# Gram results copied out of PSUM by ScalarE and VectorE, half the partitions each

## The chip, the cores and the metric

The program runs on one core of a Trainium2 chip. The metric is the device time of one execution, in microseconds. Each kernel is executed several times, and the median is compared.

## The reference

For each of 2048 samples there are 27 vectors of 128 numbers. The kernel must compute all 351 products of two different vectors of a sample, put them behind the first vector, and run the result through five dense layers, all in float32:

```python
bottom_mlp_output = bottom_output[:, 0, :]                       # (2048, 27, 128) -> (2048, 128)
interaction = jnp.einsum('bnd,bmd->bnm', bottom_output, bottom_output)
interaction_flat = interaction[:, _TRIL_R, _TRIL_C]              # 351 pairs
x = jnp.concatenate([bottom_mlp_output, interaction_flat, zero_pad], axis=1)
x = jax.nn.relu(x @ W0.T + b0)      # 480 -> 1024
x = jax.nn.relu(x @ W1.T + b1)      # -> 1024
x = jax.nn.relu(x @ W2.T + b2)      # -> 512
x = jax.nn.relu(x @ W3.T + b3)      # -> 256
return x @ W4.T + b4                # -> 1
```

## The kernel before

The samples are worked on in four chunks of 512. Before the main part, `first_gram` makes the pair products of chunk 0. Then come four bodies, `body(c)` for c from 0 to 3. Body c runs the dense layers of chunk c on TensorE, and between their matmuls it makes the pair products (grams) of chunk c+1. Body 3 has no next chunk, so it has no grams.

Every float32 operand of a dense layer is split in a high and a low float32r part. One product of a weight tile and a 128x512 activation tile is three matmuls, at lines 687, 688 and 689 (`product`). VectorE makes the splits: `split` is two instructions at lines 592 and 594, from what `relu` on ScalarE (line 414) wrote.

The grams of a chunk are made in 16 slices of 32 samples, and each slice in two halves, so 32 halves h = 0 to 31 in each of bodies 0 to 2. A half is `gram_half` on TensorE: four matmuls at line 712, which fill the two PSUM banks `gps`. There is one `gps` for all halves, so half h+1 may not start before the results of half h have been copied out. The four useful blocks of a result lie on the partition quadrants 0, 32, 64 and 96, each at another column, so that copying out takes four instructions of 32 partitions: `grams_from_psum` on ScalarE, line 382, which counts up the semaphore `grams_out`.

VectorE's share of a half is `half_point`. At an even half it is `input_parts` (lines 506 and 508: the split of the slice that is needed three slices later). At an odd half it is `half_sum` (line 524), and after every fourth slice, at h = 7, 15, 23 and 31, also `pair_products`: a transpose (line 555), two sums (559, 565) and `choose_pairs` (534). Later `transpose_pairs` on TensorE (line 725) turns these pairs, and `pairs_hi_part` (ScalarE) and `pairs_lo_part` (VectorE, line 583) move them from the PSUM bank gps to the features of the next chunk.

The order of work on every engine is written out by hand, and every engine takes its own list in order. In layer 0 a half stands behind each of the output tiles 2 to 7 (h = 0 to 5). In layer 1 the places are given by product (tile m, input tile k; k = 8 lies in the middle of the layer 2 products that follow tile m):

```python
L1_HALVES = [[1, 3, 5, 7], [0, 2, 7], [0, 3, 6, KT1], [0, 2, 7], [0, 2, 4, 7], [0, 2, KT1], [0, 2, 4, 6, KT1]]
TURNS = {(1, 4): 0, (3, 4): 1, (5, 5): 2, (MT1 - 1, 6): 3}
```

So h = 6, 7, 8 and 9 stand behind products 1, 3, 5 and 7 of tile 0, h = 10, 11 and 12 in tile 1, and so on. `layer2(c, m - 1, ...)` with its four products of m - 1 follows each tile m from 1 on. `interleave` gives ScalarE and VectorE the same order: at a place first the half, then the turn, then the output tile if k = 7.

GpSimd takes part in body 0 only: `w1_lo`, line 346, makes the low parts of the layer 1 weights, eight times.

Of the kernel before, what the change touches and what calls it, by code (L numbers as in the profile page):

```python
# [6 lines left out]
BATCH, INPUTS, EMB = 2048, 27, 128  # L7
SIZES = [1024, 1024, 512, 256]
P = 128
# [4 lines left out]
GROUP = 4  # L14
QUAD = P // GROUP
SLICE_GROUPS = 8
HALF_GROUPS = SLICE_GROUPS // 2
SCOLS = SLICE_GROUPS * GROUP * INPUTS
EVEN = INPUTS + INPUTS % 2
GCOLS = GROUP * EVEN  # L20
BANK = 512
SLICES_SUB = SUB // (GROUP * SLICE_GROUPS)
SLICES = SUBS * SLICES_SUB
HALVES = 2 * SLICES
# [38 lines left out]
def rec_program(nc, x_t, x0_t, w0, w1, w2, w3, w4, biases, b4, out):  # L63
# [5 lines left out]
    with ctx:  # L69
        def sb(name, shape, dt=f32):  # L70
            return ctx.enter_context(nc.sbuf_tensor(name, shape, dt))

        def sem(name):
            return ctx.enter_context(nc.semaphore(name))
# [28 lines left out]
        grams2 = sb("grams2", [P, 2, SLICE_GROUPS, 2, INPUTS])  # L103
# [16 lines left out]
        gps = ctx.enter_context(nc.psum_tensor("gps", [P, 2, BANK], f32))  # L120
# [13 lines left out]
        xpad_done = sem("xpad_done")  # L134
        xh_done, xl_done = sem("xh_done"), sem("xl_done")
        gram_done, grams_out, half_sums = sem("gram_done"), sem("grams_out"), sem("half_sums")
        turned_done, sums_done, pairs_done = sem("turned_done"), sem("sums_done"), sem("pairs_done")
        pairs_t, pairs_hi, pairs_lo = sem("pairs_t"), sem("pairs_hi"), sem("pairs_lo")
        dense_hi, dense_done = sem("dense_hi"), sem("dense_done")
# [6 lines left out]
        def ge(eng, s, value):  # L146

            if not (isinstance(value, int) and value <= 0):
                eng.wait_ge(s, value)
# [15 lines left out]
        def parts(g, p):  # L165

            return SLICES * (g - 1) + p + 1
# [58 lines left out]
        def pair_bank(first):  # L226
            return acc[:, 2, :] if first else gps[:, 0, :]
# [142 lines left out]
        def _(act):  # L370
            def grams_from_psum(g, h):

                n = HALVES * g + h
                act.wait_ge(gram_done, n + 1)
                if h % 2 == 0 and h >= 4:
                    act.wait_ge(half_sums, SLICES * (g - 1) + h // 2 - 1)
                at = h % 2 * HALF_GROUPS
                for q in range(GROUP):
                    rows = slice(q * QUAD, (q + 1) * QUAD)
                    src = gps[rows].rearrange("p b (g w) -> p (b g) w", w=2 * P)[:, :, 0:2 * GCOLS]  # L380
                    src = src.rearrange("p g (t c) -> p g t c", c=GCOLS)
                    last = act.activation(grams2[rows, h // 2 % 2, at:at + HALF_GROUPS, :, :],  # L382
                                          src[:, :, :, q * EVEN:q * EVEN + INPUTS], ACT.Copy)
                last.then_inc(grams_out, 1)
# [77 lines left out]
            def body(c, more):  # L462
                def on_half(h):
                    if more:
                        grams_from_psum(c + 1, h)

                def on_turn(s):
                    if more:
                        pairs_hi_part(c + 1, s)

                def on_tile(layer, m):
                    relu(c, layer, m, work[:, m % 2, :])
                    if c == 0 and layer == 0 and m < EARLY + 2:
                        w1_hi(m - EARLY)

                def after_tile(m):
                    if c == 0 and m + 2 < MT1:
                        w1_hi(m + 2)

                interleave(on_half, on_turn, on_tile, after_tile)  # L480
                for m in range(MT2):
                    relu(c, 2, m, acc[:, m, :])
                if more:
                    relu(c + 1, 0, 0, work[:, 0, :])
                for m in range(MT3):
                    relu(c, 3, m, acc[:, m, :], more)
                if more:
                    relu(c + 1, 0, 1, work[:, 1, :])
# [8 lines left out]
        def _(dve):  # L497
# [3 lines left out]
            def input_parts(g, p):  # L501
                n = SLICES * g + p
                hi, lo = xs[:, p % XSLOTS, 0, :, 0:INPUTS], xs[:, p % XSLOTS, 1, :, 0:INPUTS]
                dve.wait_ge(x_in[p % XSLOTS], 16 * (SLICES // XSLOTS * g + p // XSLOTS + 1))
                ge(dve, gram_done, 2 * (n - XSLOTS + 1))
                dve.tensor_copy(hi, by_sample(xraw, p)).then_inc(xh_done, 1)  # L506
                dve.wait_ge(xh_done, parts(g, p))
                dve.tensor_tensor(lo, by_sample(xraw, p), hi.bitcast(f32), ALU.subtract).then_inc(xl_done, 1)  # L508

            def dense_parts(g):  # L510
# [4 lines left out]
                dve.tensor_tensor(featL[:, 0, :], x0raw[:, :], featH[:, 0, :].bitcast(f32), ALU.subtract)\  # L515
                   .then_inc(dense_done, 1)

            def half_sum(g, p):

                n = SLICES * g + p  # L520
                dve.wait_ge(grams_out, 2 * (n + 1))
                ge(dve, turned_done, SUBS * g + p // SLICES_SUB)
                at = p % SLICES_SUB * SLICE_GROUPS
                dve.scalar_tensor_tensor(out=grams[:, at:at + SLICE_GROUPS, :], in0=grams2[:, p % 2, :, 0, :],  # L524
                                         scalar=0.5, in1=grams2[:, p % 2, :, 1, :], op0=ALU.mult, op1=ALU.add)\
                   .then_inc(half_sums, 1)
# [23 lines left out]
            def pair_products(g, s):  # L550

                n = SUBS * g + s
                dve.wait_ge(half_sums, SLICES_SUB * (n + 1 - SUBS))
                dve.wait_ge(sums_done, 2 * n)
                dve.transpose(turned[:, :, :], grams[:, :, :].rearrange("p g m -> p m g")).then_inc(turned_done, 1)
                dve.wait_ge(turned_done, n + 1)
                dve.wait_ge(pairs_done, n)
                full = turned[:, :, 0:INPUTS]
                dve.tensor_tensor(sums[:, 0:INPUTS * INPUTS].rearrange("p (i j) -> p i j", j=INPUTS),
                                  full, full.rearrange("p i j -> p j i"), ALU.add).then_inc(sums_done, 1)  # L560

                v = turned[:, 0, 0:APART]
                above = bass.AP(v.tensor, v.offset + APART + 1, [v.ap[0], (QUAD + 1, APART)])
                below = bass.AP(v.tensor, v.offset + QUAD * (APART + 1), [v.ap[0], (QUAD + 1, APART)])
                dve.tensor_tensor(sums[:, INPUTS * INPUTS:], above, below, ALU.add).then_inc(sums_done, 1)
                choose_pairs(n)

            def half_point(g, h):

                p = h // 2  # L570
                if h % 2 == 0:
                    if p + AHEAD < SLICES:
                        input_parts(g, p + AHEAD)
                else:
                    half_sum(g, p)
                    if p % SLICES_SUB == SLICES_SUB - 1:
                        pair_products(g, p // SLICES_SUB)
# [60 lines left out]
            def body(c, more):  # L638
                def on_half(h):
                    if more:  # L640
                        half_point(c + 1, h)
# [42 lines left out]
        def _(pe):  # L684
# [18 lines left out]
            def gram_half(g, h, turned_before):  # L703

                n, p = HALVES * g + h, h // 2
                pe.wait_ge(xl_done, parts(g, p))
                pe.wait_ge(grams_out, n)
                pe.wait_ge(pairs_lo, SUBS * g + turned_before)
                for j in range(HALF_GROUPS):
                    k = h % 2 * HALF_GROUPS + j  # L710
                    four = slice(k * GROUP, (k + 1) * GROUP)
                    last = pe.matmul(gps[:, j // 2, j % 2 * 2 * P:j % 2 * 2 * P + 2 * GCOLS],  # L712
                                     xs[:, p % XSLOTS, 0, four, :].rearrange("p b n -> p (b n)"),
                                     xs[:, p % XSLOTS, :, four, 0:EVEN], start=True, stop=True)
                last.then_inc(gram_done, 1)

            def transpose_pairs(g, s, halves_before, first=False):

                pe.wait_ge(pairs_done, SUBS * g + s + 1)
                if first:  # L720
                    ge(pe, pairs_lo, s)
                else:
                    pe.wait_ge(grams_out, HALVES * g + halves_before)
                for t in range(PAIR_TILES):
                    last = pe.transpose(pair_bank(first)[0:PAIRS_TILE, t * SUB:(t + 1) * SUB],  # L725
                                        pairs[:, t * PAIRS_TILE:(t + 1) * PAIRS_TILE], ident[:, :])
                last.then_inc(pairs_t, 1)
# [84 lines left out]
            for m in range(LEFT_AFTER, MT0 - 1):  # L812
                layer0_left(m)
            transpose_pairs(0, SUBS - 1, 0, True)
            layer0_left(MT0 - 1)

# [77 lines left out]
```

## Time and profile before

| | before |
|---|---|
| median of 3 runs | 526.73 us (525.83 to 528.72) |
| profiled execution, its own time | 528.12 us |
| its span, first to last instruction | 526.3 us |
| TensorE busy | 492.3 us, 94% |
| VectorE busy | 299.4 us, 57% |
| ScalarE busy | 239.6 us, 46% |
| GpSimd busy | 44.1 us, 8% |
| mean granted TensorE clock | 0.981 |

The engine names in the profile are PE for the matmuls and PEld for the weight loads of TensorE, DVE for VectorE, ACT for ScalarE, POOL for GpSimd. A row of the timeline gives the start within the span, the duration, the engine and the line of the kernel. Some 1.8 us of the profiled execution's time lie outside its span. A row with x4 is four instructions one right behind the other. Matmuls are pipelined, so their durations overlap, and the distance from start to start is what a matmul takes of TensorE's time.

### The profile page before, as it was taken

The page shows a single profiled execution, that of the slowest core. Times are in us where ns is not written, and L with a number is a line of the kernel's source. Part 1 is how long each engine was busy: PE and PEld are TensorE (multiplying, and loading weights), DVE is VectorE, ACT ScalarE, POOL GpSimd, SP SyncE. Part 2 cuts the span into 40 slices and gives each one's busy share as a digit, 9 for nine tenths or more (in the row PEclk, how much of TensorE's full clock was granted, in tenths as well). Part 3 has the DMA queues.
Part 4 walks back from the last instruction along what each step waited for, and adds up shares of the span by engine and source line. Part 5 has one row for each costly group of instructions (what it writes and reads, how often), then busy time and mean ns, then how long its engine had stood idle before and what let it go on. Part 6 is the DMA issues. An engine that isn't in the chain of part 4 may idle for free.

```text
span 526.3 us, 6672 instructions
## 1 busy us (share of the span) xinstructions
PE 492.3 (94%) x2480; PEld 402.8 (77%) x2480; DVE 299.4 (57%) x455; ACT 239.6 (46%) x579; POOL 44.1 (8%) x27
## 2 busy tenths in 40 slices
PE   6999769897999999899999999899999999999996
PEld 5999766675777878687777878687787888888874
DVE  3596897867545756757554666767464634101124
ACT  2887266574663335645554425745645322101111
POOL 0336340130310000000000000000000000000000
PEclk9999779999999989999999999999999999999998
DMA  7895046566537322454344232354332200424200
GB/s 272 327 375 182 7 128 222 176 220 230 181 130 244 106 63 70 153 192 158 149 142 154 81 101 68 127 203 147 112 128 81 81 1 0 141 100 161 80 0 2
DMA packets 17456, 72.28 MB, mean 137 GB/s; under 512 B 2448, under 2 KB 2448, under 8 KB 13328
## 3 DMA queue, kind: packets, MB, share of 16 engines
q1 hardware_dynamic: 17424, 71.86, 38.8%
q8 instruction: 20, 0.33, 0.3%
q14 instruction: 12, 0.10, 0.1%
HBM read 63.45 MB, written 8.40 MB: 137 GB/s over the span
## 4 chain that ended last, share of the span: by engine, by line
PE 77%; DVE 10%; issue 7%; ACT 4%; DMA 1%; SPq 0%; DVEq 0%; ACTq 0%
PE work L687 15%; PE work L688 15%; PE work L689 15%; PE gps L712 9%; PE acc L687 6%; PE acc L688 6%; PE acc L689 6%; PE acc L699 2%; DVE xs L506 1%; ACT grams L382 1%; ACT grams L398 1%; DMA xraw<-x_t 1%; DVE h2h L592 1%; PE gps L699 1%; PE gps L725 1%
## 5 line engine op out<-in xcount | busy, mean ns | idle before, releaser
L382 ACT ACTIVATE grams<-gps 32x216 f32<-32x216 f32 x384 | 131.0, 341 | 82.0 <-PE gps L712 78.4
L687 PE MATMUL work<-h1h,w1s 128*128 128x512 f32 x256 | 102.4, 400 | 0.0
L688 PE MATMUL work<-h1h,w1s 128*128 128x512 f32 x256 | 101.7, 397 | 0.0
L689 PE MATMUL work<-h1l,w1s 128*128 128x512 f32 x256 | 100.8, 394 | 0.0
L414 ACT ACTIVATE act_out<-work,bias 128x512 f32<-128x512 f32 (+1 forms) x64 | 42.3, 662 | 116.3 <-PE work L689 111.7
L712 PEld LDWEIGHTS gps<-xs 128*128 128x128 f32 x384 | 54.6, 193 | 38.9 <-issue 27.3
L712 PE MATMUL gps<-xs 128*128 128x224 f32 x384 | 62.3, 285 | 17.0 <-issue 9.6
L687 PE MATMUL work<-featH,w0l 117*128 117x512 f32 (+5 forms) x160 | 59.9, 374 | 4.0 <-ACT act_out L421 3.7
L592 DVE CAST h2h<-act_out 128x512 fp32r<-128x512 f32 x40 | 19.2, 481 | 75.7 <-ACT act_out L414 75.7
L524 DVE SCALAR_TENSOR_TENSOR grams<-grams 128x216 f32<-128x216 f32 x48 | 20.3, 422 | 73.5 <-ACT grams L382 72.7
L689 PE MATMUL work<-featL,w0h 117*128 117x512 f32 (+5 forms) x160 | 58.5, 366 | 0.0
L688 PE MATMUL work<-featH,w0h 117*128 117x512 f32 (+5 forms) x160 | 58.5, 366 | 0.0
L689 PEld LDWEIGHTS work<-h1l,w1s 128*128 128x128 f32 x256 | 48.1, 188 | 11.3
L508 DVE TENSOR_TENSOR xs<-xraw,xs 128x864 fp32r<-128x864 f32 x48 | 55.0, 1145 | 1.7
L687 PEld LDWEIGHTS work<-h1h,w1s 128*128 128x128 f32 x256 | 48.4, 189 | 8.6
L688 PEld LDWEIGHTS work<-h1h,w1s 128*128 128x128 f32 x256 | 48.4, 189 | 8.0
L687 PE MATMUL acc<-h2h,w2l 128*128 128x512 f32 x128 | 50.7, 396 | 0.0
L688 PE MATMUL acc<-h2h,w2h 128*128 128x512 f32 x128 | 50.7, 396 | 0.0
L689 PE MATMUL acc<-h2l,w2h 128*128 128x512 f32 x128 | 50.5, 395 | 0.0
L592 DVE CAST h1h<-act_out 128x512 fp32r<-128x512 f32 (+1 forms) x48 | 21.5, 448 | 41.9 <-ACT act_out L414 41.8
L687 PEld LDWEIGHTS work<-featH,w0l 117*128 117x128 f32 (+2 forms) x160 | 32.8, 205 | 8.3 <-ACT act_out L421 4.1
L688 PEld LDWEIGHTS work<-featH,w0h 117*128 117x128 f32 (+2 forms) x160 | 33.0, 206 | 4.0
(68 smaller groups left out, 582.4 us busy)
## 6 DMA issues: line engine op xcount, KB each, us to landing
xraw<-x_t SPq DMA_DIRECT2D x64, 432.0 KB, 5.1
w1s<-w_parts SPq DMA_DIRECT2D x24, 1024.0 KB, 4.8
w_parts<-w1s SPq DMA_DIRECT2D x8, 1024.0 KB, 5.7
stage<-w_t SPq DMA_DIRECT2D x8, 512.0 KB, 7.1
w0raw<-w_t SPq DMA_DIRECT2D x4, 512.0 KB, 7.2
w2raw<-w_t SPq DMA_DIRECT2D x4, 512.0 KB, 6.5
x0raw<-x_t SPq DMA_DIRECT2D x4, 256.0 KB, 3.6
w3raw<-w_t SPq DMA_DIRECT2D x1, 512.0 KB, 6.6
```

What stands on the lines that cost most here:

```text
L382: last = act.activation(grams2[rows, h // 2 % 2, at:at + HALF_GROUPS, :, :], src[:, :, :, q * EVEN:q * EVEN + INPUTS], ACT.Copy)
L398: last = act.activation(dst, src[:, :, :, q * INPUTS:(q + 1) * INPUTS], ACT.Copy)
L414: act.activation(act_out[:, slot(layer, m, more), cols], bank[:, cols], ACT.Relu, bias=bias[:, row:row + 1]).then_inc(relu_done, 1)
L506: dve.tensor_copy(hi, by_sample(xraw, p)).then_inc(xh_done, 1)
L508: dve.tensor_tensor(lo, by_sample(xraw, p), hi.bitcast(f32), ALU.subtract).then_inc(xl_done, 1)
L524: dve.scalar_tensor_tensor(out=grams[:, at:at + SLICE_GROUPS, :], in0=grams2[:, p % 2, :, 0, :], scalar=0.5, in1=grams2[:, p % 2, :, 1, :] ...
L592: dve.tensor_copy(hi, full).then_inc(hi_done, 1)
L687: pe.matmul(dst, wl, ah, start=start, stop=False)
L688: pe.matmul(dst, wh, ah, start=False, stop=False)
L689: return pe.matmul(dst, wh, al, start=False, stop=stop)
L699: last = pe.matmul(first_banks(p)[:, k // HALF_GROUPS, at:at + GROUP * INPUTS], four.rearrange("p b n -> p (b n)"), four[:, :, 0:INPUTS], ...
L712: last = pe.matmul(gps[:, j // 2, j % 2 * 2 * P:j % 2 * 2 * P + 2 * GCOLS], xs[:, p % XSLOTS, 0, four, :].rearrange("p b n -> p (b n)"), x ...
```

## The change

ScalarE copies only the quadrants 0 and 32 of a half. The quadrants 64 and 96 are copied by VectorE, in the new `lower_from_psum`, which is the first thing in `half_point`. A new semaphore `lower_out` counts the copied halves. `gram_half`, `transpose_pairs` and `half_sum` now wait for it as well as for `grams_out`. The pair products of chunk 0 (`first_from_psum`) keep their four copies on ScalarE.

```diff
         gram_done, grams_out, half_sums = sem("gram_done"), sem("grams_out"), sem("half_sums")
+        lower_out = sem("lower_out")
...
             def grams_from_psum(g, h):
...
-                for q in range(GROUP):
+                for q in range(GROUP // 2):
...
+            def lower_from_psum(g, h):
+
+                n = HALVES * g + h
+                dve.wait_ge(gram_done, n + 1)
+                if h % 2 == 0 and h >= 4:
+                    dve.wait_ge(half_sums, SLICES * (g - 1) + h // 2 - 1)
+                at = h % 2 * HALF_GROUPS
+                for q in range(GROUP // 2, GROUP):
+                    rows = slice(q * QUAD, (q + 1) * QUAD)
+                    src = gps[rows].rearrange("p b (g w) -> p (b g) w", w=2 * P)[:, :, 0:2 * GCOLS]
+                    src = src.rearrange("p g (t c) -> p g t c", c=GCOLS)
+                    last = dve.tensor_copy(grams2[rows, h // 2 % 2, at:at + HALF_GROUPS, :, :],
+                                          src[:, :, :, q * EVEN:q * EVEN + INPUTS])
+                last.then_inc(lower_out, 1)
+
             def half_sum(g, p):
 
                 n = SLICES * g + p
                 dve.wait_ge(grams_out, 2 * (n + 1))
+                dve.wait_ge(lower_out, 2 * (n + 1 - SLICES))
...
             def half_point(g, h):
 
                 p = h // 2
+                lower_from_psum(g, h)
...
             def gram_half(g, h, turned_before):
...
                 pe.wait_ge(grams_out, n)
+                ge(pe, lower_out, n - HALVES)
...
             def transpose_pairs(g, s, halves_before, first=False):
...
                     pe.wait_ge(grams_out, HALVES * g + halves_before)
+                    pe.wait_ge(lower_out, HALVES * (g - 1) + halves_before)
```

## Rows read from the trace of the kernel before

**Rows 1.** The page, part 1: busy time of each engine.

```profile
PE 492.3 (94%) x2480; PEld 402.8 (77%) x2480; DVE 299.4 (57%) x455; ACT 239.6 (46%) x579; POOL 44.1 (8%) x27
```

**Rows 2.** The page, part 4: the chain that ended last, by engine.

```profile
PE 77%; DVE 10%; issue 7%; ACT 4%; DMA 1%; SPq 0%; DVEq 0%; ACTq 0%
```

**Rows 3.** The page, part 5: busy, mean ns, idle time before.

```profile
L382 ACT ACTIVATE grams<-gps 32x216 f32<-32x216 f32 x384 | 131.0, 341 | 82.0 <-PE gps L712 78.4
```

**Rows 4.** Timeline, TensorE, body 1: start us, us, engine, line, operands, [idle before].

```profile
199.03 0.60 PE L712 MATMUL gps<-xs 128*128 128x224 f32 x4
199.47 0.40 PE L687 MATMUL work<-featH,w0l 128*128 128x512 f32 x1
...
202.28 0.60 PE L712 MATMUL gps<-xs 128*128 128x224 f32 x4
...
211.06 0.68 PE L712 MATMUL gps<-xs 128*128 128x224 f32 x4 [0.26 <-issue]
...
213.28 0.68 PE L712 MATMUL gps<-xs 128*128 128x224 f32 x4
213.79 0.40 PE L687 MATMUL work<-h1h,w1s 128*128 128x512 f32 x1
...
215.49 0.68 PE L712 MATMUL gps<-xs 128*128 128x224 f32 x4
...
279.78 0.68 PE L712 MATMUL gps<-xs 128*128 128x224 f32 x4
```

**Rows 5.** Timeline, ScalarE, the same stretch.

```profile
213.99 1.40 ACT L382 ACTIVATE grams<-gps 32x216 f32<-32x216 f32 x4 [0.81 <-PE gps L712]
```

**Rows 6.** Timeline, VectorE, the same body.

```profile
215.43 0.38 DVE L524 SCALAR_TENSOR_TENSOR grams<-grams 128x216 f32<-128x216 f32 x1 [2.44 <-ACT grams L382]
...
219.84 0.60 DVE L506 CAST xs<-xraw 128x864 fp32r<-128x864 f32 x1
...
221.46 0.38 DVE L524 SCALAR_TENSOR_TENSOR grams<-grams 128x216 f32<-128x216 f32 x1
221.75 0.42 DVE L592 CAST h2h<-act_out 128x512 fp32r<-128x512 f32 x1
...
222.82 0.42 DVE L513 CAST featH<-x0raw 128x512 fp32r<-128x512 f32 x1
...
223.88 0.60 DVE L506 CAST xs<-xraw 128x864 fp32r<-128x864 f32 x1
```

**Rows 7.** Groups by form: VectorE's read of PSUM.

```profile
L583 DVE TENSOR_TENSOR featL<-gps,featH 117x384 fp32r<-117x384 f32 x12 | 6.6, 554 | 3.9 <-ACT featH L406 3.8
```

**Rows 8.** Timeline, body 0: VectorE's end and the TensorE group that it released.

```profile
124.35 0.55 DVE L583 TENSOR_TENSOR featL<-gps,featH 117x384 fp32r<-117x384 f32 x1
125.05 0.68 PE L712 MATMUL gps<-xs 128*128 128x224 f32 x4 [1.98 <-DVE featL L583]
```

**Rows 9.** Timeline, body 0: VectorE beside a GpSimd subtraction.

```profile
94.22 2.54 POOL L346 TENSOR_TENSOR w1s<-stage,w1s 128x1024 fp32r<-128x1024 f32 x1 [18.86 <-ACT w1s L440]
...
94.39 2.64 DVE L592 CAST h2h<-act_out 128x512 fp32r<-128x512 f32 x1
...
116.87 2.43 DVE L565 TENSOR_TENSOR sums<-turned 128x13 f32<-128x13 f32 x1
...
141.78 3.08 DVE L559 TENSOR_TENSOR sums<-turned 128x729 f32<-128x729 f32 x1
```

**Rows 10.** Timeline, TensorE, starts behind its two longest idle times before body 3.

```profile
56.23 0.58 PE L687 MATMUL work<-featH,w0l 128*128 128x256 f32 x1 [3.70 <-ACT act_out L421]
...
70.92 1.17 PE L712 MATMUL gps<-xs 128*128 128x224 f32 x4 [4.07 <-issue]
```

**Rows 11.** Windows: us, PE busy, PEld, DVE, ACT, POOL, PEclk, DMA share, GB/s.

```profile
56.00:62.00 6.00, 5.76 (x27) 5.77 (x28) 4.34 (x10) 2.70 (x6) 1.30 (x1) 0.50 0.00 0
...
71.00:76.00 5.00, 5.00 (x24) 5.00 (x25) 4.97 (x4) 3.44 (x9) 4.18 (x2) 0.50 0.28 91
...
125.00:127.00 2.00, 1.96 (x11) 1.71 (x12) 0.00 (x0) 1.20 (x4) 0.00 (x0) 1.00 1.01 419
```

## Prediction

> **What bounds the kernel now.** I read the page's busy times first, then the chain, then the costliest groups, and then the timeline around the halves. TensorE is busy 94% of the span [rows 1] and is 77% of the chain that ended last [rows 2], so only what moves TensorE's matmuls moves the end. The copies that the change touches are ScalarE's largest group: 384 instructions, 131.0 us, 341 ns each [rows 3]. ScalarE is busy under half of the time, so its total says nothing. The question is which wait ends last before a half starts on TensorE.
>
> A half that waits for nothing has its next product 0.44 us behind its start (199.03 to 199.47), and one that had to wait has it at 0.51 (213.28 to 213.79), so a wait costs 0.07 beyond its own length [rows 4]. A matmul of 512 columns takes 0.234 start to start: a layer 0 tile has twelve of them, from 199.47 to 202.28 [rows 4]. So a product takes 0.70, and from 213.79 two of them end at 215.19. The next half starts only at 215.49: a stall of 0.30 [rows 4]. ScalarE's four copies begin at 213.99, 0.71 behind the half's start, and end at 215.39, 0.10 before the next half [rows 5]. So where only two products lie between halves, the four copies (1.40) set the pace, and the half waits. In body 1 I count 15 such stalls, from the half at 211.06 to that at 279.78, with the two turns at tiles 1 and 3: thirteen of 0.28 to 0.34, one of 0.42 and one of 1.00 (h = 10, with only one product before it), 5.69 us in all, and with 15 x 0.07 = 1.05 it is **6.7 us per body**. VectorE makes TensorE wait in none of them. Body 2 shows the same pattern. This is all that halving ScalarE's copies can win there: 2 x 0.35 instead of 4 x 0.35 would end 0.70 earlier, more than the 0.30 that is missing.
>
> **What the change costs on VectorE.** Two copies of 216 elements per half are added, 192 in all. None of the trace's rows is a plain copy from PSUM by VectorE. From PSUM it took 554 ns for 384 elements [rows 7]; from SBUF the same number of elements as ours, 216, took 0.38 (line 524) [rows 6]. With one element per cycle as in rows of this kind, (0.554 - 0.38) / 168 = 1.04 ns an element, both rows lie on one line, and so I take 0.38. Between instructions I add 0.04 (my choice; on ScalarE it is 0.01, 1.40 / 4 against 0.341 [rows 3, 5]), so a pair costs 0.84. Low bound: a single-source copy inside SBUF runs faster, 0.42 for 512 elements and 0.60 for 864 [rows 6], by which slope one of 216 takes 0.27, about 0.30 with its gap. High bound: 0.50 each, near the whole 0.55 of the longer PSUM read.
>
> The Trainium skill (VectorE: DVE Perf Modes, "Why PSUM operands drop a tier") says that a float32 operand in PSUM keeps a copy at one element per cycle, which rules out my low bound; no run here shows it yet. Its cycle table ("The TRN2 errata" section) gives (120 + 216) / 0.96 = 350 ns as an estimate, with which a body would lose some 6 us in place of the 8 below.
>
> **Where VectorE stands when a half is ready.** This decides. `lower_from_psum` stands in VectorE's own order, behind everything that earlier places gave it, and the half after next cannot start before it. Its other work per place, start to start [rows 6]: `half_sum` 0.30 (221.46 to 221.75); `half_sum` and `pair_products` together 4.41 (215.43 to 219.84); `input_parts` 1.62 (219.84 to 221.46); `split` 1.07 (221.75 to 222.82); the dense parts 1.06 (to 223.88). Before, a half did not wait for any of it except for inputs made three slices ahead. From VectorE's end to the half it releases are 0.15 (124.90 to 125.05) [rows 8], so from the end of the pair's 0.84 slot 0.11.
>
> I write R for the time at which a half's results are ready, 0.71 behind its start. With n products between, the next half could start at R - 0.20 + 0.70 n.
>
> *Halves 7 to 11* (two products apart, h = 10 one). At h = 6 VectorE copies (0.84) and splits an input (1.62), so it reaches half 7 at V, 0.62 late, and half 8 is held to V + 0.95, a stall of 0.36. Then VectorE does copy 7 (0.84), sum and pair products (4.41), copy 8 (0.84): 6.09, and half 9 starts at V + 6.20. Free it would start at V + 0.95 + 1.91 = V + 2.86. **Stall 3.34.** Next, input parts 1.62 and copy 9: half 10 at V + 8.66 against 7.41, stall 1.25. Then sum, the split of tile (1,0), the dense parts, copy 10 (0.30 + 1.07 + 1.06 + 0.84): half 11 at V + 11.93 against 10.57, stall 1.36. Then input parts and copy 11: the turn at V + 14.39 against 13.84, stall 0.55.
>
> *Halves 15 to 18.* After half 15 VectorE does copy, sum, pair products, the split of tile (1,2), copy 16: 7.16, and half 17 starts at R + 7.27. TensorE has three products, half 16, three products: free at R + 4.44. **Stall 2.83**, and 0.55 at half 18 behind the next input parts.
>
> *Halves 23 to 25.* The same chain, 7.27, against five products, a half, two products: 5.14. **Stall 2.13.**
>
> *The rest.* Half 6 stands two products behind the last tile of layer 0, whose relu and split VectorE must do before copy 5: 1.40 by the same account. Half 22 gets 0.36, as half 8. Half 31's pair products have eight products before the turn needs them, no stall. In layer 0 a tile and a half take 3.25, and VectorE needs per pair of them 2 x (1.07 + 0.84) + 1.62 + 0.30 = 5.74 of 6.50: covered. All others are covered too, since ScalarE's 0.70 and VectorE's 0.84 then both fit.
>
> Sum: 1.40 + 0.36 + 3.34 + 1.25 + 1.36 + 0.55 + 2.83 + 0.55 + 0.36 + 2.13 = 14.1, and ten times 0.07: **14.8 us per body against 6.7 now, +8.1**. So the stalls of 0.30 mostly go, and fewer but long ones come. The same account with a copy at 0.30 gives +5.0, with 0.50 +11.2. It needs no idle VectorE on average: the engine is 57% busy [rows 1] and stays under 70%.
>
> **Body 0** has the same three places and more. GpSimd's subtractions hold VectorE instructions: the cast at 94.39 took 2.64 instead of 0.42, ending with GpSimd's at 96.76, the sum at 116.87 took 2.43 instead of some 0.17, that at 141.78 took 3.08 instead of 1.51 [rows 9]. The second and third lie inside pair products 1 and 2 and the first between copies 9 and 10, so all three (2.2 + 2.2 + 1.6 = 6.0) now stand before a half; some 1 us of it costs already (the 1.98 of idle at 125.05 [rows 8]). The Trainium skill (SBUF — State Buffer, "Who interferes with whom") says VectorE and GpSimd hold a shared port pair against each other for whole instructions, and that a one-source instruction outside the two-port modes is not held: then the new copies themselves are not, only what stands before them. Layer 0 there has 256 columns, a tile and half took 2.2, VectorE's 5.1 per pair of tiles exceeds 4.4: +1.2 over four tiles. Together 8.1 + 6.0 - 1.0 + 1.2 = 14.3.
>
> **The clock.** Behind idle times of 3.70 and 4.07 [rows 10] the granted clock was 0.50 (1.2 GHz) for at least 6 and 5 us; behind 1.98 it stayed 1.00 (2.4 GHz) [rows 8, 11]. At half clock at most half the time is lost: some 2.5 us an event. In body 0 the stall at half 17 becomes 2.8 + 2.2 = 5, so I add one event: +2.2, taking the part of it that matmuls fill. Whether 3.34 in the steady bodies does it, no row tells; it lies between the two. I leave it out of the sum. The Trainium skill (TensorE: Matmul & The Clock Gate, "The HAM clock gate") also has the clock at half behind an idle stretch, as rows 10 and 11 show.
>
> **Sum.** 2 x 8.1 + 14.3 + 2.2 = 32.7. On the profiled execution, 528.1 + 32.7 = 560.8 (span 559); on the median, which is 1.4 lower, **559 us**.
>
> **Rivals.**
> - *A: as forecast, and the clock falls in bodies 1 and 2 too*, behind half 9 at least: 2 x 2.5 more, with a second event in body 0 some 567.
> - *B: the copies collide.* Both engines read the same two banks at once. If one waits for the other, the pair takes up to 0.70 longer. By the account's slope (3.1 us a body for 0.16 us a pair), 3 x 13 more: about 597. Nothing in the trace has both engines on `gps` at once; that they read different partitions speaks against it.
> - *C: faster.* VectorE would be in time at the halves, and then only the 6.7 us a body go: 527 - 20 = 507. For it: VectorE is idle 43% of the span and idled 2.44 before 215.43 [rows 6]. Against: it idles elsewhere than at pair products. It decides in favour of C only if the chain of 6.09 behind half 7 takes under 2.8, that is if pair products were under 0.8 instead of some 4.0, or stood behind the next halves' copies.
> - *D: no change*, gains equal to losses: it needs the long stalls at a fourth of their size, at most 3.5 us a body beside the small ones. Only copies at nearly no time and half the chain would do that.
>
> **How the numbers follow.** The forecast (546 to 563) 0.70, A 0.17, B 0.04, C 0.04, D 0.02, and slower by less than forecast 0.03. Low end: copies at 0.30 and body 0 at 9, 2 x 5.0 + 9 = 19: 546; I go to 544. High end: copies at 0.50 with the clock of A, 2 x (11.2 + 2.5) + 22 = 49: 576. Faster or slower means by over 0.5%, 2.6 us, about what a measurement of this kernel can tell from no change.
>
> **What would show it.** ScalarE's line 382 halves to 192 instructions and some 65 us. VectorE has 192 new copies of about 0.38. In body 1 TensorE has idle times before line 712 of about 3.2, 2.7 and 2.0 us at halves 9, 17 and 25, released by VectorE, and the 0.30s at halves 7, 21, 28, 29 and 30 are gone. If the copies took under 0.2, or if TensorE did not wait behind pair products, the prediction would be wrong. The last body and everything before the first half must be as long as before.

## The result and the profile after

The changed kernel takes 574.9 us (median of 4 runs, 573.59 to 575.65) against 527.3 us (4 runs): a ratio of 1.090, 95% interval 1.086 to 1.094. It is slower by 48 us. The forecast was 559 with a range of 544 to 576, so the time lies in the range, 1 us below its upper end, and above the 546 to 563 that had the largest chance. The profiled execution took 573.59 us, with a span of 571.8 and a mean granted clock of 0.933 instead of 0.981.

Part 1 and three groups of part 5 of the page of the changed kernel:

```profile
PE 508.8 (89%) x2480; PEld 420.9 (74%) x2480; DVE 377.3 (66%) x647; ACT 174.2 (30%) x387; POOL 44.4 (8%) x27
...
L383 ACT ACTIVATE grams<-gps 32x216 f32<-32x216 f32 x192 | 65.3, 340 | 173.4 <-PE gps L731 172.0
...
L731 PE MATMUL gps<-xs 128*128 128x224 f32 x384 | 67.0, 301 | 47.0 <-DVE grams L530 46.8
...
L530 DVE COPY grams<-gps 32x216 f32<-32x216 f32 x192 | 73.8, 384 | 39.7 <-PE gps L731 36.5
```

Against [rows 1, 3], ScalarE's copies are halved in number and no slower (340 ns, before 341). VectorE's are 192 of 384 ns. VectorE is 66% busy, so it is not full. But TensorE now idles 47.0 us before the halves (line 731), and 46.8 of it end with a VectorE copy.

The timeline shows how. TensorE in body 1 of the changed kernel, the halves 6 to 10 (starts 233.53, 235.45 for half 7, 237.83 for half 8, 243.19 for half 9 and 245.73 for half 10) and then halves 17 and 25; and half 25 of body 2:

```profile
233.53 0.68 PE L731 MATMUL gps<-xs 128*128 128x224 f32 x4 [1.49 <-DVE grams L530]
...
237.83 0.68 PE L731 MATMUL gps<-xs 128*128 128x224 f32 x4 [0.29 <-DVE grams L530]
...
243.19 1.17 PE L731 MATMUL gps<-xs 128*128 128x224 f32 x4 [3.27 <-DVE grams L530]
...
245.73 1.17 PE L731 MATMUL gps<-xs 128*128 128x224 f32 x4
...
271.30 1.17 PE L731 MATMUL gps<-xs 128*128 128x224 f32 x4 [2.95 <-DVE grams L530]
...
299.13 0.68 PE L731 MATMUL gps<-xs 128*128 128x224 f32 x4 [2.24 <-DVE grams L530]
...
430.24 0.76 PE L731 MATMUL gps<-xs 128*128 128x224 f32 x4 [2.25 <-DVE grams L530]
```

VectorE in the same stretch: copies of half 7, half sum, pair products (lines 572 to 551), copies of half 8:

```profile
236.79 0.78 DVE L530 COPY grams<-gps 32x216 f32<-32x216 f32 x2
237.66 0.38 DVE L541 SCALAR_TENSOR_TENSOR grams<-grams 128x216 f32<-128x216 f32 x1
238.08 1.95 DVE L572 STREAM_TRANSPOSE turned<-grams 128x864 f32<-128x864 f32 x1
240.06 1.41 DVE L576 TENSOR_TENSOR sums<-turned 128x729 f32<-128x729 f32 x1
241.39 0.17 DVE L582 TENSOR_TENSOR sums<-turned 128x13 f32<-128x13 f32 x1
241.60 0.52 DVE L551 COPY pairs<-sums 128x351 f32<-128x351 f32 x1
242.15 0.78 DVE L530 COPY grams<-gps 32x216 f32<-32x216 f32 x2
```

Half 8 was ready at 238.5, 0.71 behind its start at 237.83, but its copies on VectorE began only at 242.15, behind the pair products. Half 9 started 0.26 behind their end (242.93). And the half that started at 243.19 takes 1.17 instead of 0.68: TensorE is at half clock. The windows tell it (columns: stretch, us, busy of PE, PEld, DVE, ACT and POOL with counts, then PEclk, DMA share, GB/s); the first two follow halves 9 and 17 of body 1, the third half 25 of body 1, the fourth half 25 of body 2:

```profile
242.00:250.00 8.00, 6.74 (x22) 5.25 (x23) 7.57 (x16) 2.05 (x5) 0.00 (x0) 0.57 0.64 244
270.00:278.00 8.00, 6.70 (x24) 5.72 (x24) 5.82 (x12) 1.36 (x4) 0.00 (x0) 0.57 0.20 56
298.00:304.00 6.00, 4.87 (x25) 4.11 (x26) 4.22 (x9) 1.49 (x4) 0.00 (x0) 1.00 0.00 0
430.00:436.00 6.00, 5.76 (x22) 4.79 (x23) 3.35 (x6) 1.17 (x3) 0.00 (x0) 0.72 0.01 3
```

For the split of the loss I read from each timeline when the first half starts and when the first matmul of layer 4 starts in each body. Body 0 is from the first half, bodies 1 and 2 from layer 4 to layer 4:

| us | body 0 | body 1 | body 2 |
|---|---|---|---|
| before | 121.5 | 121.5 | 119.2 |
| changed | 142.7 (+21.2) | 133.7 (+12.2) | 131.9 (+12.7) |

From there to the last layer 4 both kernels take 94.8, and before the first half 64.8 and 64.5. So all the loss lies in the bodies that have halves. The kernel before takes 2.3 us more for body 1 than for body 2; there the windows show half clock for some 3.4 us right behind the layer 4 of body 0 (0.72 granted from 188 to 194), and none in body 2.

### The profile page after: what moved, and what is told of

Read it like the earlier page. It is cut to its first block and busy times, and to the rows that moved or that the text cites. A ratio compares the mean times of both kernels' runs of the same rounds, so it can differ in the third digit from the quotient of the medians.

```text
span 571.8 us, 6809 instructions
## 1 busy us (share of the span) xinstructions
PE 508.8 (89%) x2480; PEld 420.9 (74%) x2480; DVE 377.3 (66%) x647; ACT 174.2 (30%) x387; POOL 44.4 (8%) x27
## 5 line engine op out<-in xcount | busy, mean ns | idle before, releaser
L383 ACT ACTIVATE grams<-gps 32x216 f32<-32x216 f32 x192 | 65.3, 340 | 173.4 <-PE gps L731 172.0
L731 PEld LDWEIGHTS gps<-xs 128*128 128x128 f32 x384 | 60.7, 211 | 66.2 <-issue 60.5
L731 PE MATMUL gps<-xs 128*128 128x224 f32 x384 | 67.0, 301 | 47.0 <-DVE grams L530 46.8
L705 PE MATMUL work<-h1h,w1s 128*128 128x512 f32 x256 | 108.8, 425 | 0.0
L706 PE MATMUL work<-h1h,w1s 128*128 128x512 f32 x256 | 107.7, 421 | 0.0
L707 PE MATMUL work<-h1l,w1s 128*128 128x512 f32 x256 | 106.3, 415 | 0.0
L530 DVE COPY grams<-gps 32x216 f32<-32x216 f32 x192 | 73.8, 384 | 39.7 <-PE gps L731 36.5
L707 PEld LDWEIGHTS work<-h1l,w1s 128*128 128x128 f32 x256 | 51.9, 203 | 12.7
L610 DVE CAST h2h<-act_out 128x512 fp32r<-128x512 f32 x40 | 17.0, 424 | 65.6 <-ACT act_out L415 65.6
L705 PEld LDWEIGHTS work<-h1h,w1s 128*128 128x128 f32 x256 | 52.1, 204 | 9.3
L706 PEld LDWEIGHTS work<-h1h,w1s 128*128 128x128 f32 x256 | 52.2, 204 | 8.8
L610 DVE CAST h1h<-act_out 128x512 fp32r<-128x512 f32 (+1 forms) x48 | 19.2, 401 | 36.1 <-ACT act_out L415 36.1
```

The source lines that it names most:

```text
L530: last = dve.tensor_copy(grams2[rows, h // 2 % 2, at:at + HALF_GROUPS, :, :], src[:, :, :, q * EVEN:q * EVEN + INPUTS])
L610: dve.tensor_copy(hi, full).then_inc(hi_done, 1)
L705: pe.matmul(dst, wl, ah, start=start, stop=False)
L706: pe.matmul(dst, wh, ah, start=False, stop=False)
L707: return pe.matmul(dst, wh, al, start=False, stop=stop)
```

## The experiments

All are the changed kernel with one edit, except where said. Times are medians beside runs of the kernel before on the same chip (526.8, 527.8 and 526.9 in the three groups).

**1. Pair products cut short.** The pairs of chunks 1 to 3 are left out, and the instructions that would make them are kept short in place.

```diff
-                dve.transpose(turned[:, :, :], grams[:, :, :].rearrange("p g m -> p m g")).then_inc(turned_done, 1)
+                dve.transpose(turned[:, 0:1, :], grams[:, :, 0:1].rearrange("p g m -> p m g")).then_inc(turned_done, 1)
...
-                dve.tensor_tensor(sums[:, 0:INPUTS * INPUTS].rearrange("p (i j) -> p i j", j=INPUTS),
-                                  full, full.rearrange("p i j -> p j i"), ALU.add).then_inc(sums_done, 1)
+                dve.tensor_tensor(sums[:, 0:INPUTS], full[:, 0, :], full[:, 0, :], ALU.add).then_inc(sums_done, 1)
```

> The changed kernel, but pair_products works on one column group only: the transpose takes 1 of 27 blocks and the first sum 27 of 729 elements (so the pairs of chunks 1 to 3 are not computed; the other instructions, all waits and the places stay). Backlog theory (a half waits behind the 4 us of pair products in VectorE's order): the block shrinks from 4.0 to about 1.2 us, the stalls of 3.4, 3.1 and 2.4 us per body go, the clock stays at 1.00 in bodies 1 and 2, and the time falls from 575 to 525 to 535. Rival (the copies themselves or both engines reading the same banks cost it): most of the loss stays, 560 or more.

539.4 us, ratio 1.023 (1.020 to 1.027). The bodies take 130.1, 123.0 and 122.4: 35 of the 48 us are gone, though all 192 copies and all waits are still there. The expectation of 525 to 535 was too low by at least 4 us: body 0 keeps 8.6 of its loss, and bodies 1 and 2 keep 1.5 and 3.2. In body 1 half 9, the one that waited for pair products 0, is now at 224.81 (half 8 at 222.37, half 10 at 227.35):

```profile
222.37 0.68 PE L730 MATMUL gps<-xs 128*128 128x224 f32 x4 [0.31 <-DVE grams L530]
224.81 0.68 PE L730 MATMUL gps<-xs 128*128 128x224 f32 x4 [0.35 <-DVE grams L530]
227.35 0.68 PE L730 MATMUL gps<-xs 128*128 128x224 f32 x4 [1.15 <-DVE grams L530]
```

Idle 0.35 where it was 3.27. What stands ahead of the copies is the main cause, and the two engines' reading of the same banks is not.

**2. Copies cut short.** Each copy of VectorE takes 27 of its 216 elements, so most of the quadrants 64 and 96 is left uncopied.

```diff
-                    last = dve.tensor_copy(grams2[rows, h // 2 % 2, at:at + HALF_GROUPS, :, :],
-                                          src[:, :, :, q * EVEN:q * EVEN + INPUTS])
+                    last = dve.tensor_copy(grams2[rows, h // 2 % 2, at:at + 1, 0:1, :],
+                                          src[:, 0:1, 0:1, q * EVEN:q * EVEN + INPUTS])
```

> The changed kernel, but each of VectorE's copies takes 27 of its 216 elements (so the grams of partitions 64 to 127 are mostly not copied); the waits and the place in VectorE's order stay. Backlog theory: a pair costs about 0.44 instead of 0.84 us, the stalls at halves 9, 17 and 25 stay at about 2.8, 2.4 and 1.7 us since they are made of pair products, and the time is 545 to 558. Rival (the duration of 192 copies, 74 us on VectorE, is the cost): the time falls to that of before or below, 510 to 530.

552.1 us, ratio 1.048 (1.043 to 1.053), as the backlog theory had it. TensorE still idles 2.72, 2.39 and 1.72 before halves 9, 17 and 25 of body 1. With the copies cut short about half of the loss stays (25 of 48 us). The copies' own length matters too, since a late half waits for the pair products and for one or two pairs of copies behind them; so what experiments 1 and 2 win, 35 and 23 us, adds up to more than the loss. The page of this run also gives the price per element of a copy from PSUM:

```profile
L530 DVE COPY grams<-gps 32x27 f32<-32x27 f32 x192 | 36.0, 188 | 46.6 <-PE gps L731 43.5
```

The 189 elements fewer save 196 ns, 1.04 ns each.

**3. The split three to one at every half.** ScalarE copies three quadrants, VectorE one.

```diff
+        ON_VECTOR, FIRST_Q = [0, 1, 2, 3, 4, 5, 6, 7, 8, 9, 10, 11, 12, 13, 14, 15, 16, 17, 18, 19, 20, 21, 22, 23, 24, 25, 26, 27, 28, 29, 30, 31], 3
...
-                for q in range(GROUP // 2):
+                for q in range(FIRST_Q if h in ON_VECTOR else GROUP):
...
-                for q in range(GROUP // 2, GROUP):
+                for q in range(FIRST_Q, GROUP):
```

`ON_VECTOR` lists the halves of which VectorE takes a part, here all, and `FIRST_Q` is its first quadrant.

> The split is 3 to 1: at every half ScalarE copies quadrants 0 to 64 (1.05 us) and VectorE only quadrant 96. By my account with the measured 0.26 us from VectorE to TensorE a body loses 5.5 us in place of 9.6 on waits: half 9 still waits 3.1, half 17 2.8, half 25 2.1. With the clock falls and body 0's extra some 550 to 558. If VectorE's total time (a half less of copies, 37 us) were what counts, half of the loss would go: 551; if pair products ahead of copies count, no more than a third.

556.5 us, ratio 1.056 (1.052 to 1.061), in the range given. Before halves 9, 17 and 25 of body 1 TensorE idles 2.98, 2.73 and 2.06, against 3.27, 2.95 and 2.24 with two copies. The result does not tell the two readings named there apart: 40% of the loss is gone, between a third and a half, and bodies differ in clock falls as well. The three idle times speak for the queue: they fell by only 0.2 to 0.3 each.

**4. Pair products in two pieces.**

```diff
                 dve.transpose(turned[:, :, :], grams[:, :, :].rearrange("p g m -> p m g")).then_inc(turned_done, 1)
+
+            def pair_sums(g, s):
+
+                n = SUBS * g + s
...
                 lower_from_psum(g, h)
-                if h % 2 == 0:
+                if h % (2 * SLICES_SUB) == 1 and h > 1:
+                    half_sum(g, p)
+                    pair_sums(g, h // (2 * SLICES_SUB) - 1)
+                elif h % 2 == 0:
...
                         pair_products(g, p // SLICES_SUB)
+                        if h == HALVES - 1:
+                            pair_sums(g, SUBS - 1)
```

Here `pair_products` ends behind the transpose, and `pair_sums` is the rest of it.

> The changed kernel with pair_products cut in two: the transpose stays at halves 7, 15 and 23, the sums and the choice of pairs move behind the copies and the half sum of halves 9, 17 and 25. Same instructions. If the backlog of VectorE's work counts and not the length of one block, the stalls move (half 9 from 3.4 to 1.5, half 11 to some 3.4, half 17 from 3.1 to 1.0, the turns 1 and 2 up to 1.3 and 2.3) and their sum stays: 0.5 us less per body by my account, with one clock fall less per body 2 us more, so 566 to 573. If the block is the cause, the time falls to 550 or below.

567.5 us, ratio 1.077 (1.072 to 1.081), in the range given. The stalls moved. The halves 8, 9, 10 and 11 and the turn of body 1 (230.72, 233.99, 236.53, 241.97, 244.41; line 754 is the turn):

```profile
230.72 0.68 PE L740 MATMUL gps<-xs 128*128 128x224 f32 x4 [0.31 <-DVE grams L530]
233.99 0.68 PE L740 MATMUL gps<-xs 128*128 128x224 f32 x4 [1.19 <-DVE grams L530]
236.53 0.94 PE L740 MATMUL gps<-xs 128*128 128x224 f32 x4 [1.16 <-DVE grams L530]
241.97 0.68 PE L740 MATMUL gps<-xs 128*128 128x224 f32 x4 [1.91 <-DVE grams L530]
244.41 0.56 PE L754 MATMUL gps<-ident,pairs 128*117 128x128 f32 x3 [0.35 <-DVE grams L530]
```

Half 11 idled 1.91, less than the 3.4 I expected: I had not followed that with TensorE at half clock behind half 10 VectorE gets some time back. Cutting the block in two wins 7 us, not the loss, so the length of one block is not the cause. Body 1, with one clock fall, took 129.3; body 2, with two, 133.6. The fall in body 1 came behind half 10, with idle times of only 1.19 and 1.16 ahead of it (granted clock 0.52 from 237.0 to 240.3).

**5. Fillers for the clock.** Nine more matmuls ahead of halves 9, 17 and 25, in the time in which TensorE waits anyway. Their results are overwritten.

```diff
             def gram_half(g, h, turned_before):
...
+                if h in (9, 17, 25):
+                    m = {9: 0, 17: 3, 25: 5}[h]
+                    pe.wait_ge(relu_done, nth(g - 1, 1, m))
+                    for _ in range(9):
+                        pe.matmul(work[:, (m + 1) % 2, :], w0h[:, 0, 0:P], featH[:, 0, :], start=True, stop=True)
```

First with ten, at halves 9 and 17 only:

> The changed kernel with ten more matmuls of 512 columns on TensorE ahead of half 9 and of half 17, into the bank of work that is free there (their results are overwritten): they fill 2.3 of the 3.4 and 3.1 us that TensorE waits there anyway. If the half clock behind these waits is a cost of its own: the clock stays at 1.00 in bodies 1 and 2, some 2 to 3 us are won behind half 17, little behind half 9 because VectorE is late at halves 10 and 11 in any case, and the time is 562 to 570. If the stalls alone are the loss and the clock only goes with them: 574 to 576.

573.1 us, ratio 1.087 (1.082 to 1.092): outside what either reading gave, between their 570 and 574. The trace shows why. In body 1 half 25 came at 90.1 us behind the start of the body (the layer 4 of the body before) instead of 91.9, but the clock, full behind halves 9 and 17, now fell behind half 25, and from there to layer 4 it took 43.3 instead of 41.8. So about 3.4 us at half clock cost 1.5. Behind half 9 nothing was won: TensorE now idled 1.17 and 1.33 for VectorE before halves 10 and 11, which at half clock it had not. Then, with all three filled, beside the changed kernel itself:

> The changed kernel itself, unchanged, beside the next one on the same chip: 574 to 576.

> The changed kernel with nine extra 512-column matmuls ahead of half 9, half 17 and half 25 in each of bodies 0 to 2. With fillers at halves 9 and 17 only, TensorE came to half 25 of body 1 1.8 us earlier, but the clock then fell behind half 25 and took 1.5 back. If the clock is a cost of its own, the fall behind half 25 is gone too, and bodies 1 and 2 are each 2 to 3 us shorter than in the changed kernel: 567 to 571. If not: no change against it.

575.9 us for the changed kernel (ratio 1.093, 1.089 to 1.096) and 565.9 with the fillers (1.073, 1.069 to 1.076): 10 us, with 81 matmuls more, and 1 us below the 567 to 571 expected. Body 1 is shorter by 5.7 us and body 2 by 2.1, where 2 to 3 were given for each. The windows of body 1, first of the changed kernel on this chip, then with fillers:

```profile
205.60:341.50 135.90, 123.79 (x564) 100.19 (x564) 100.52 (x180) 38.46 (x91) 0.00 (x0) 0.92 0.34 116
```

```profile
203.60:333.90 130.30, 121.78 (x592) 98.05 (x592) 100.64 (x180) 38.43 (x91) 0.00 (x0) 1.00 0.35 121
```

With the clock at 1.00 in the whole body it takes 130.3. The halves 9, 10 and 11 of it stand much as the prediction's account has them, 1.33 and 1.50 late at 10 and 11 (1.25 and 1.36 forecast):

```profile
238.11 0.68 PE L736 MATMUL gps<-xs 128*128 128x224 f32 x4 [1.26 <-DVE grams L530]
240.66 0.68 PE L736 MATMUL gps<-xs 128*128 128x224 f32 x4 [1.16 <-DVE grams L530]
244.08 0.68 PE L736 MATMUL gps<-xs 128*128 128x224 f32 x4 [1.33 <-DVE grams L530]
```

(A stall, counted from start to start as in the prediction, is 0.17 longer than the idle time in the brackets, since a matmul's row lasts 0.40 and the next one could start 0.23 behind its start.)

**6. GpSimd's share in body 0.** Its subtractions are cut to 16 of 1024 columns, in the changed kernel and in the kernel before. The low parts of the layer 1 weights are zeros otherwise. The cut shows the lines of the changed kernel.

```diff
-                pool.tensor_tensor(w1s[:, m % 2, 1, :], stage[:, m % 2, :], w1s[:, m % 2, 0, :].bitcast(f32),
+                if m < 2:
+                    pool.memset(w1s[:, m % 2, 1, 16:].bitcast(f32), 0.0).then_inc(w1_clear, 1)
+                    pool.wait_ge(w1_clear, m + 1)
+                pool.tensor_tensor(w1s[:, m % 2, 1, 0:16], stage[:, m % 2, 0:16], w1s[:, m % 2, 0, 0:16].bitcast(f32),
```

> The changed kernel, but GpSimd's eight subtractions of layer 1 weights in body 0 take 16 of 1024 columns (the low parts of these weights are zeros otherwise; slots 0 and 1 are cleared by a memset). Theory: body 0 lost 21 us where bodies 1 and 2 lost 12 and 13, because VectorE instructions that GpSimd holds stand ahead of copies. Then body 0 comes down to a loss like the others', 8 to 10 us are won, 564 to 567. Rival: body 0 loses more because its layer 0 has half the columns, whatever GpSimd does: at most 3 us are won, 572 or more.

> The kernel before with the same cut of GpSimd's subtractions (low parts of the layer 1 weights mostly zero). VectorE has slack there and TensorE waits for it in body 0 twice only (1.0 and 2.1 us, pairs_lo): 2 to 5 us are won, 522 to 525. If GpSimd's holds cost TensorE the same with either kernel, what is won is as much as with the changed kernel.

557.6 us (ratio 1.059, 1.054 to 1.063) and 523.3 (0.993, 0.990 to 0.995). Body 0 takes 128.8 and 117.8. So GpSimd's work cost body 0 of the changed kernel 14.0 us and that of the kernel before 3.7. I had expected 8 to 10 for the first, and the time is below the 564 to 567 given. Without that work, body 0 of the changed kernel is 10.9 above that of the kernel before, near the 12.2 and 12.7 of the other bodies. A part that I had not counted lies in layer 0 of the changed kernel's body 0, at its half 2. GpSimd, VectorE and then TensorE, here and at half 17 (134.59):

```profile
69.42 5.11 POOL L347 TENSOR_TENSOR w1s<-stage,w1s 128x1024 fp32r<-128x1024 f32 x2 [6.40 <-ACT w1s L441]
```

```profile
70.03 2.23 DVE L507 CAST xs<-xraw 128x864 fp32r<-128x864 f32 x1
72.30 3.15 DVE L509 TENSOR_TENSOR xs<-xraw,xs 128x864 fp32r<-128x864 f32 x1
...
76.14 0.78 DVE L530 COPY grams<-gps 32x216 f32<-32x216 f32 x2
```

```profile
77.18 1.17 PE L731 MATMUL gps<-xs 128*128 128x224 f32 x4 [3.17 <-DVE grams L530]
...
134.59 1.16 PE L731 MATMUL gps<-xs 128*128 128x224 f32 x4 [5.13 <-DVE grams L530]
```

The two instructions of one `input_parts` took 5.4 us instead of 1.6 beside two of GpSimd's subtractions, and the copies behind them were late by as much. With GpSimd's work cut, half 2 starts 3.79 behind half 1 instead of 6.92, and half 17 5.71 behind half 16 instead of 7.83. The copies themselves were not held: a pair at 148.11, inside a subtraction from 146.59 to 149.03, took the usual 0.78.

**7. VectorE helps only where it is free.** The queue theory can be turned round: keep ScalarE's four copies, and let VectorE take some only where its list has nothing long ahead and the next half stands two products on.

```diff
+        ON_VECTOR, FIRST_Q = [6, 7, 20, 21, 27, 28, 29], 3
+
+        def lowered(g, h):
+
+            return len(ON_VECTOR) * (g - 1) + sum(x < h for x in ON_VECTOR)
...
-                for q in range(GROUP // 2):
+                for q in range(FIRST_Q if h in ON_VECTOR else GROUP):
...
             def lower_from_psum(g, h):
 
+                if h not in ON_VECTOR:
+                    return
...
-                for q in range(GROUP // 2, GROUP):
+                for q in range(FIRST_Q, GROUP):
...
-                ge(pe, lower_out, n - HALVES)
+                ge(pe, lower_out, lowered(g, h))
```

> VectorE copies one quadrant (96 to 127) and only of halves 6, 7, 20, 21, 27, 28 and 29, where the next half stands two products on and VectorE has no pair products ahead of it; ScalarE copies three quadrants there and all four elsewhere. Backlog theory: seven of the fifteen stalls per body (those of halves 7, 8, 21, 22, 28, 29 and 30) go at 0.37 us each, 2.6 us a body, so 519 to 521 against 527. Rival (any wait on VectorE costs more than it gives): 527 or more.

518.9 us, ratio 0.984 (0.982 to 0.987): faster than both kernels, and a tenth of a us below the 519 to 521 that the account gave. The halves 6 to 11 of body 1:

```profile
204.68 0.68 PE L739 MATMUL gps<-xs 128*128 128x224 f32 x4 [0.26 <-issue]
206.60 0.62 PE L739 MATMUL gps<-xs 128*128 128x224 f32 x4
208.48 0.61 PE L739 MATMUL gps<-xs 128*128 128x224 f32 x4
210.63 0.68 PE L739 MATMUL gps<-xs 128*128 128x224 f32 x4
212.85 0.68 PE L739 MATMUL gps<-xs 128*128 128x224 f32 x4 [0.84 <-issue]
215.07 0.68 PE L739 MATMUL gps<-xs 128*128 128x224 f32 x4
```

Halves 7 and 8 start 1.92 and 1.88 behind the one before, no longer 2.22; halves 9 and 11, which still wait for four copies of ScalarE, start 2.15 and 2.22 behind theirs. From the first half to the last turn, bodies 1 and 2 are 2.6 us shorter each, as forecast, and body 0 is 1.7 shorter. That makes 6.8 us in the profiled executions (1.3%), where the medians differ by 7.9. These executions also differ by 3.2 us before the first half, where the edit changes nothing and where two executions of the changed kernel differ by 1.5.

The same with two copies each, at halves 6, 20, 27, 28 and 29:

> The split is 2 to 2 again, but VectorE copies only in halves 6, 20, 27, 28 and 29. By my account the stalls of halves 7, 21, 28, 29 and 30 go, five times 0.37 = 1.85 us a body, so 5 us less than before: 521 to 523. If the three-to-one split were what made the other version faster, this one would not be faster than before.

523.2 us, ratio 0.994 (0.991 to 0.996), at the edge of the 521 to 523 given. From the first half to the last turn, bodies 1 and 2 are 1.9 and 2.0 shorter than before (1.85 forecast). So an even split is no fault in itself.

## Why the prediction was right, and where its sum was short

**The mechanism** held: the half waits for VectorE behind the pair products, and ScalarE's group halved. The forecast had stalls of 1.40, 0.36, 3.34, 1.25, 1.36 and 0.55 for halves 6, 8, 9, 10, 11 and the turn. With the clock at 1.00 those of body 1 measured 1.64, 0.53, 3.5 (partly filled), 1.33, 1.50 and 0.5.

The copies took 384 ns where 0.38 us was written. The Trainium skill (VectorE: DVE Perf Modes, "Why PSUM operands drop a tier") says that a float32 operand in PSUM keeps a copy at one element per cycle, and this trace agrees, with 384 ns for 216 elements and the 1.04 ns an element of experiment 2. The 350 ns that the prediction estimated from the Trainium skill's cycle table ("The TRN2 errata" section of the same page) are a tenth short. By the account's own slope below 0.38 (3.1 us for 0.24 us a pair) they would have made a body lose some 7 us, not the 6 that were written.

Rival B (the engines hold each other up at the banks) is out: both engines' copies kept their times, and experiment 1 removed most of the loss with both still reading. Rivals C (faster) and D (no change) are out by the time.

**That the time lies in the range is in part luck.** The forecast proper ended at 563, and rival A stood at 567. The upper end of 576 was built with copies of 0.50 us, which did not come. Its three terms (11.2 of waits and 2.5 of clock in each steady body, 22 in body 0) are near to what was measured, but for other reasons, told in what follows.

**The sum** was 32.7 us for 45.5 in span. By its terms:

- *The waits of a steady body*, +8.1. From the first half to the last turn the kernel before takes 96.6 in bodies 1 and 2, with the clock at 1.00. The kernel with fillers takes 107.0 in body 1, at 1.00 too, and as much in body 2. So the waits cost 10.4, 2.3 more than forecast. The stalls of that body, from start to start, add up to 16.0 instead of 14.1: half 17 stalls 3.13 (2.83 forecast), half 25 2.41 (2.13), half 6 1.64 (1.40), and half 2, which was taken to be covered, 0.24. The mis-sized part is what stands around the copies: I took 0.15 us from VectorE's end to TensorE [rows 8], and behind a copy it measured 0.26; from the half sum to the next copies it was 4.49, not 4.41. Such gaps stand before every late half.
- *The clock in bodies 1 and 2*, left out of the sum and made rival A. Rival A came true. In the profiled execution the clock fell behind idle times of 3.27 and 2.95 in both bodies and behind 2.25 at half 25 of body 2, but not behind 2.24 at half 25 of body 1. Above the 107.0 of the full clock this cost 1.8 us in body 1 and 2.4 in body 2, near A's 2.5 a body. But A priced one event, behind half 9, at 2.5. That one cost between nothing and 0.6, for VectorE is what TensorE waits for there. Behind half 17, 6.8 us at half clock cost some 2 and 3.4 us cost 0.8; behind half 25, 3.4 us cost 1.5.
- *Body 0*, forecast at 14.3 and 2.2 for one clock event, measured 21.2, so 4.7 more. Experiment 6 splits it. From half 6 on, GpSimd's work cost the changed kernel 9.6 us and the kernel before 4.0, with the clock falls that it brings: 5.6 net, where 6.0 less 1.0 was written. From half 0 to half 6, in layer 0, it cost the changed kernel 4.4 and the kernel before nothing. What failed is that I counted three held instructions in layer 1 and left out those in layer 0, though [rows 11] have GpSimd busy 4.18 of the 5 us from 71 on.

These three are some 4.5, 4.2 and 4.7 us too little; outside these bodies the trace of the changed kernel is 0.6 shorter. Which part of body 0's loss is clock and which is waiting was not separated. Nor does any run show why the clock fell behind some idle times and not behind others. It is not the same in each execution: body 1 of the changed kernel is 12.2 longer than before in one profile and 14.5 in another.

## What to carry to other kernels

Before work is moved to an engine because it is idle 43% of the time, look at where it stands in that engine's own list: a short copy that gates the next matmuls is as late as the longest work queued ahead of it. Add the durations ahead of it, place by place, against the time until the result is needed; here that account gave the stalls of the steady bodies within some 0.3 us at full clock, while the busy shares said nothing. It missed where something outside it changed the durations: half 2 of body 0 beside GpSimd, and half 11 of experiment 4 at half clock. The same account shows where a split does pay: seven halves out of 32, one quadrant each, gave 1.6% (some 1.3% by the account of the bodies), and two quadrants of all 32 cost 9%.

## What was not expected of the hardware

- The granted clock fell to 0.50 behind idle times of 2.25 and 2.95 us before a half, and did not fall behind one of 2.24 us in the same execution. A second profile of the same kernel has it the other way round: a fall behind 2.24 at half 25 of body 1, none behind 2.28 at half 25 of body 2. In experiment 4 it fell behind two of 1.19 and 1.16. The length of one idle time alone does not tell.
- Nine extra matmuls in an idle time, nine times over, made the kernel faster: with these 81, 565.9 us against 575.9.
- A half clock was nearly free where TensorE waited for VectorE right afterwards. In body 1 half 10 starts 2.54 us behind half 9 at half clock and 2.55 at full clock, and half 12 10.89 and 10.90 behind it. In a second execution, where the clock fell only with half 10, half 12 came 11.54 behind.
- The same eight GpSimd subtractions cost 3.7 us of body 0 in one order of VectorE's work and 14.0 in the other.
